# First layer of a two-layer kernel: the channel mixing moved from the input of the big product to its result

## The reference, cut to what matters

```python
agg_w = einsum('bk,koi->boi', att, weight[..., 0])     # one 64 x 64 matrix per batch
agg_b = att @ bias_k                                   # one number per batch and channel
xf    = einsum('boi,bih->boh', agg_w, x) + agg_b[:, :, None]
h     = relu(layernorm(xf @ gw1.T + gb1)); gates = h @ gw2.T + gb2; top 2 of 8, capacity
out   = x + xf @ weight.T + lora(xf, gates)            # tmp = xf @ lora_A
# second layer: convolution along the 1024, condition bias, products with Wq, Wk, W, A, mixed experts
```

## Time and profile before

| what | value |
|---|---|
| median of 3 runs | 1356.77 us (1352.99 to 1357.81) |
| profiled execution | 1357.82 us, of it the span of the trace 1356.0 |
| PE busy | 1305.2 us (96%), mean granted clock 0.987 |
| DVE busy | 814.2 us (60%); 7 or 8 tenths in phase A, 4 or 5 in phase B |
| ACT, POOL busy | 301.2 us (22%), 243.4 us (18%) |
| DMA | mean 93 GB/s over the span |

### The profile page before, as it was taken

The page is one execution under the profiler, slowest core; times in us unless marked ns, Lnnn a source line. Parts: engine busy times, 40 slices in busy tenths (PEclk is TensorE's granted clock), DMA queues, the critical chain, the costliest instruction groups (busy, mean ns, idle before and its releaser), DMA issues.

```text
span 1356.0 us, 21754 instructions
## 1 busy us (share of the span) xinstructions
PE 1305.2 (96%) x7429; PEld 1206.8 (89%) x7429; DVE 814.2 (60%) x2039; ACT 301.2 (22%) x510; POOL 243.4 (18%) x145
## 2 busy tenths in 40 slices
PE   6799999999999997879999999999999999999999
PEld 6699999999999996768988988989889889898897
DVE  7888888888888885545454454454544544545442
ACT  5422332223322331311111111111111111111110
POOL 5422223222222222400100101001001010010010
PEclk9899999999999998889999999999999999999999
DMA  5422222232222235542443433524434335244320
GB/s 200 168 71 90 86 70 70 73 100 72 70 70 90 85 87 160 163 98 67 99 99 73 109 82 84 113 68 99 100 75 106 83 84 112 69 100 98 80 52 31
DMA packets 100295, 125.74 MB, mean 93 GB/s; under 512 B 5168, under 2 KB 80944, under 8 KB 100272
## 3 DMA queue, kind: packets, MB, share of 16 engines
q1 hardware_dynamic: 100272, 125.43, 34.5%
HBM read 71.62 MB, written 53.80 MB: 92 GB/s over the span
## 4 chain that ended last, share of the span: by engine, by line
PE 77%; DVE 12%; issue 3%; ACT 3%; DMA 1%; DVEq 0%; ACTq 0%; SPq 0%
PE ps L998 22%; PE ps L999 21%; PE ps L1000 21%; PE ps L1123 6%; PE ps L1041 3%; PE ps L1124 2%; DVE gate L762 2%; ACT row L543 2%; DVE whole L726 2%; DVE whole L729 1%; DVE row L767 1%; PE ps L1042 1%; DVE mixs L707 1%; DMA x_round<-row 1%; ACT lhs_h L534 1%
## 5 line engine op out<-in xcount | busy, mean ns | idle before, releaser
L998 PE MATMUL ps<-weights,lhs_h 128*128 128x396 f32 (+2 forms) x1792 | 635.0, 354 | 11.8 <-DVE row L748 6.0
L999 PE MATMUL ps<-weights,lhs_h 128*128 128x396 f32 (+2 forms) x1792 | 624.9, 349 | 0.0
L1000 PE MATMUL ps<-weights,lhs_l 128*128 128x396 f32 (+2 forms) x1792 | 624.3, 348 | 0.0
L998 PEld LDWEIGHTS ps<-weights,lhs_h 128*128 128x128 f32 x1792 | 339.8, 190 | 36.9 <-issue 11.4
L1000 PEld LDWEIGHTS ps<-weights,lhs_l 128*128 128x128 f32 x1792 | 339.2, 189 | 20.6
L999 PEld LDWEIGHTS ps<-weights,lhs_h 128*128 128x128 f32 x1792 | 339.6, 190 | 19.6
L506 POOL TENSOR_TENSOR xo<-row,on_all 128x512 f32<-128x512 f32 x64 | 84.1, 1339 | 676.1 <-DMA out_x<-xo 669.3
L1123 PE MATMUL ps<-conv_hl,part_h 128*128 128x256 f32 x512 | 123.9, 332 | 2.4 <-DVE part_l L886 2.4
L465 POOL TENSOR_TENSOR part_l<-xo,part_h 128x1024 fp32r<-128x1024 f32 x31 | 83.1, 2681 | 210.5 <-ACT part_h L527 210.5
L1124 PE MATMUL ps<-conv_hl,part_l 128*128 128x128 f32 x512 | 115.3, 225 | 0.0
L534 ACT ACTIVATE lhs_h<-whole 128x512 fp32r<-128x512 f32 x64 | 40.5, 633 | 319.1 <-DVE whole L729 319.1
(11 more groups left out here) (144 smaller groups left out, 1283.0 us busy)
## 6 DMA issues: line engine op xcount, KB each, us to landing
spill<-row SPq DMA_DIRECT2D x32, 584.5 KB, 3.8
row<-spill SPq DMA_DIRECT2D x31, 584.5 KB, 5.8
z<-x_round SPq DMA_DIRECT2D x32, 516.0 KB, 4.0
xo<-in_x SPq DMA_DIRECT2D x32, 512.0 KB, 4.1
x_round<-row SPq DMA_DIRECT2D x64, 256.0 KB, 5.4
out_x<-xo SPq DMA_DIRECT2D x31, 512.0 KB, 2.7
staging<-in_w SPq DMA_DIRECT2D x8, 832.0 KB, 5.5
bias_in<-cond_rows SPq DMA_DIRECT2D x63, 64.0 KB, 3.9
```

The costliest lines, as they stand in the source:

```text
L998: pe.matmul(out_ap, lhs[0], rhs[0], start=first, stop=False, skip_group_check=True)
L999: pe.matmul(out_ap, lhs[0], rhs[1], start=False, stop=False, skip_group_check=True)
L1000: return pe.matmul(out_ap, lhs[1], rhs[0], start=False, stop=last, skip_group_check=True)
```

## The change

- The host lays x out twice: `xt`, transposed in blocks so that a tile of it is `lhs_h`/`lhs_l` after a split, and `xr`, rows of 1184 columns: `gb1`, 128 zeros, and x in the order of `row`.
- `main` of a tile works on plain x. Its three banks are split again (`y_high` by ACT, `y_low` by DVE, into `yh`, `yl`), and `mix(t, k)` multiplies them with the mixing matrix as the stationary operand, three matmuls of 396 columns for each bank, into banks of their own (BM0).
- `column_sums` multiplies each slice of the weights with a matrix of ones while the first tile is computed; ACT keeps the sums (`wsum`), and for each tile makes `biased` = wsum times the channel's bias. POOL's `row_init` adds it to the loaded `xr` in `row`; `evict` (DVE) adds the mixed banks to that. `lhs_a`, `x_keep`, `main_bank` and the x bias load go.
- `x_low` moves from POOL to DVE; the split of chunk N_LB0 moves from DVE to POOL; the five aside chunks are spread over tiles 1 to 5.
- The condition's small matmuls stand between the slices of tile 0, on PE and ACT; the warming matmuls ahead of tile 0 are gone.

The core of the diff (blank lines left out):

```diff
-        BY0 = (4, 5, 7)
+        BY0, BM0, BC = (4, 5, 7), (1, 2, 3), (0, 6)
...
-        by_pool = (3, 6, N_CONV, N_LB1, N1, N1 + 1, N1 + 2, N1 + 4, N1 + 6)
+        after0 = {N1 + 2: last0 - 2, N1 + 3: last0 - 1, N1 + 5: last0}
+        by_pool = (3, 6, N_LB0, N_CONV, N_LB1, N1, N1 + 1, N1 + 2, N1 + 4, N1 + 6)
...
-        aside = {0: (N_LB0, N_CONV), 1: (N_LB1, N1), TILES - 2: (N1 + 1,)}
+        aside, HEAD = {1: N_LB0, 2: N_CONV, 3: N_LB1, 4: N1, 5: N1 + 1}, 6
...
+            def load_xt(t, u):
+                sp.dma_start(xo[:, u, :], a["xt"][bass.ts(t, P), :]).then_inc(xt_in[u], 16)
+            def load_xr(t, u):
+                sp.dma_start(row[:, u, 0:OUT0], a["xr"][bass.ts(t, P), :]).then_inc(xr_in[u], 16)
...
+            load_xt(0, 0)
+            chunk(0)
             sp.dma_start(cbuf[:, 0:CPACK], a["cpack"]).then_inc(cond_in, 16)
+            chunk(1)
+            chunk(2)
...
+            chunk(3)
+            load_xt(1, 1)
+            chunk(4)
...
+            sp.wait_ge(*low_of(3))
+            load_xr(0, 0)
...
+                once, ahead, thrice = counts(t + 1, t + 3, t * 3 + 3)
+                if later(t, 1) and before_end(t, 1):
+                    left, = counts((it + u) * 16)
+                    sp.wait_ge(spilled[1 - u], left)
                     sp.sem_inc(passed_sp, 1)
...
+                    load_xr(t + 1, 1 - u)
+                if before_end(t, 4):
+                    sp.wait_ge(x_lo, ahead)
+                    sp.sem_inc(passed_sp, 1)
+                    load_xt(t + 4, u)
+                if isinstance(t, int) and t + 1 in aside and t > 0:
+                    chunk(aside[t + 1])
...
+                sp.wait_ge(mix_read, thrice)
+                sp.sem_inc(passed_sp, 1)
+                sp.wait_ge(counted, once)
+                sp.sem_inc(passed_sp, 1)
+                sp.dma_start(spill[bass.ts(t, P), :], row[:, u, HG:END]).then_inc(spilled[u], 16)
...
+            def row_init(t, u, it):
+                pool.wait_ge(biased_ready, t + 1)
+                pool.wait_ge(xr_in[u], it * 16 + 16)
+                if later(t, 1):
+                    pool.wait_ge(counted, t)
+                pool.tensor_tensor(row[:, u, 0:OUT0], row[:, u, 0:OUT0], biased[:, :], ALU.add).then_inc(row_ready, 1)
...
+                if before_end(t, 1):
                     mix_product(t + 1)
...
+                    row_init(t + 1, 1 - u, it + u)
+                if isinstance(t, int) and t in aside:
+                    split_lo(aside[t])
...
             def x_high(t, u, it):
...
+                act.wait_ge(xt_in[u], it * 16 + 16)
...
+                    act.wait_ge(main_done, t * 3 - 3)
+                act.activation(lhs_h[:, u, :, :], xo[:, u, :].rearrange("p (j t) -> p j t", j=J),
+                               ACT.Copy).then_inc(x_hi, 1)
+            def y_high(t, k):
+                act.wait_ge(main_done, t * 3 + k + 1)
+                if later(t, 1):
+                    act.wait_ge(mix_done, t * 3 - 2 + k)
+                act.activation(yh[:, k, :], ps[:, BY0[k], 0:BANK0], ACT.Copy).then_inc(y_hi, 1)
+            def bias_of(t):
+                if later(t, 1):
+                    act.wait_ge(row_ready, t)
+                    act.sem_inc(passed_act, 1)
+                act.activation(biased[:, :], wsum[:, 0:OUT0], ACT.Copy,
+                               scale=aggc[:, bass.ds(t, 1)]).then_inc(biased_ready, 1)
...
+            x_high(0, 0, 0)
+            split_hi(0)
...
+            act.activation(h1, ps[:, BC[0], 0:B], ACT.Gelu, bias=cb0).then_inc(cond_act, 1)
+            split_hi(1)
...
+            split_hi(4)
             x_high(1, 1, 0)
...
+            for k in range(3):
+                act.wait_ge(wsum_done, k + 1)
+                act.activation(wsum[:, BANK0 * k:BANK0 * k + BANK0], ps[:, BM0[k], 0:BANK0],
+                               ACT.Copy).then_inc(wsum_ready, 1)
+            y_high(0, 0)
+            y_high(0, 1)
+            act.wait_ge(aggc_ready, 2)
+            act.wait_ge(wsum_ready, 3)
+            bias_of(0)
...
+            def phase_a(t, u, it):
+                if at(t, TILES - 1):
+                    root(t)
+                    y_high(t, 2)
+                    return
+                y_high(t, 2)
+                if before_end(t, 2):
+                    x_high(t + 2, u, it + 1)
+                y_high(t + 1, 0)
+                bias_of(t + 1)
+                root(t)
+                y_high(t + 1, 1)
+                if isinstance(t, int) and t in aside:
+                    split_hi(aside[t])
...
+            def x_low(t, u):
+                dve.wait_ge(x_hi, t + 1)
+                dve.tensor_tensor(lhs_l[:, u, :, :], xo[:, u, :].rearrange("p (j t) -> p j t", j=J),
+                                  f32(lhs_h[:, u, :, :]), ALU.subtract).then_inc(x_lo, 1)
+            def y_low(t, k):
+                dve.wait_ge(y_hi, t * 3 + k + 1)
+                dve.tensor_tensor(yl[:, k, :], ps[:, BY0[k], 0:BANK0], f32(yh[:, k, :]),
+                                  ALU.subtract).then_inc(y_lo, 1)
...
+            def evict(t, u, k):
+                dve.wait_ge(mix_done, t * 3 + k + 1)
+                if k == 0:
+                    dve.wait_ge(row_ready, t + 1)
...
+                dve.tensor_tensor(row[:, u, lo:hi], ps[:, BM0[k], 0:hi - lo], row[:, u, lo:hi],
+                                  ALU.add).then_inc(mix_read, 1)
...
+                y_low(t, 2)
+                if before_end(t, 2):
+                    x_low(t + 2, u)
+                evict(t, u, 0)
+                y_low(t + 1, 0)
+                evict(t, u, 1)
+                evict(t, u, 2)
+                if at(t, TILES - 2):
+                    mix_matrix(t + 1)
                 route(t, u)
-                if at(t, 1):
-                    links["n"] += MIX_LINKS
+                y_low(t + 1, 1)
+                if not at(t, TILES - 2):
+                    mix_matrix(t + 1)
...
-            main_bank(TILES - 1, 1, 1)
+            evict(TILES - 1, 1, 1)
+            evict(TILES - 1, 1, 2)
...
+            def cond(step):
+                if step == 0:
+                    pe.wait_ge(cond_in, 16)
+                    pe.matmul(ps[:, BC[0], 0:B], cw0, emb_t, start=True, stop=True).then_inc(cond_pe, 1)
+                elif step == 1:
+                    pe.wait_ge(cond_act, 1)
+                    pe.matmul(ps[:, BC[1], 0:B], cw1, h1, start=True, stop=True).then_inc(cond_pe, 1)
+                elif step == 2:
+                    pe.wait_ge(cond_act, 2)
+                    pe.matmul(ps[0:B, BC[0], 64:64 + KATT], h2, cw2, start=True, stop=True).then_inc(cond_pe, 1)
+                elif step == 4:
+                    pe.wait_ge(consts_in, 16)
+                    pe.wait_ge(cond_dve, 4)
+                    pe.transpose(ps[0:KATT, BC[1], 64:64 + B], att, eye[0:B, 0:B]).then_inc(cond_pe, 1)
+                    pe.matmul(ps[0:B, BC[1], 128:128 + C], emb_t, ctx_w, start=True, stop=True).then_inc(cond_pe, 1)
+                    pe.matmul(ps[:, BC[0], 128:128 + TILES * KATT], batch_part, wbuf[0:B, 0:TILES * KATT],
+                              start=True, stop=True).then_inc(cond_pe, 1)
+                elif step == 6:
+                    pe.wait_ge(cond_dve, 6)
+                    pe.matmul(ps[:, BC[1], 192:192 + B], bias_k, attT, start=True, stop=True).then_inc(cond_pe, 1)
...
+            def column_sums(j):
+                for k in range(3):
+                    for s in range(2):
+                        mm = pe.matmul(ps[:, BM0[k], 0:BANK0], ones[:, :], w0[:, k, j, s, :],
+                                       start=(j == 0 and s == 0), stop=(j == J - 1 and s == 1), skip_group_check=True)
+                    if j == J - 1:
+                        mm.then_inc(wsum_done, 1)
...
+                if j0 == 0 and k == 0:
+                    pe.wait_ge(x_hi, t + 1)
...
+                    pe.wait_ge(y_lo, t * 3 - 2 + k)
...
+            def mix(t, k):
+                if k == 0:
+                    pe.wait_ge(mix_ready, t * 2 + 2)
+                pe.wait_ge(y_lo, t * 3 + k + 1)
+                if later(t, 1):
+                    pe.wait_ge(mix_read, t * 3 - 2 + k)
+                elif k == 0:
+                    pe.wait_ge(wsum_ready, 3)
+                split_product(ps[:, BM0[k], 0:BANK0], (mix_h, mix_l), (yh[:, k, :], yl[:, k, :])).then_inc(mix_done, 1)
+            pe.wait_ge(zeroed, 4)
+            for j in range(J):
+                for k in range(3):
+                    main(0, 0, k, j, j + 1)
+                column_sums(j)
+                cond(j)
...
+                main(t + 1, 1 - u, 0)
+                for k in range(3):
+                    mix(t, k)
+                main(t + 1, 1 - u, 1)
+                if at(t, TILES - 2):
+                    mix(t + 1, 0)
+                main(t + 1, 1 - u, 2)
...
+    rows = f["x"].reshape(B * C, D)
+    a = {"xt": rows.reshape(TILES, P, J, P).transpose(0, 3, 2, 1).reshape(TILES * P, D),
```

(2 more changed lines are left out.)

424 lines of the change are left out of this document (121 added, 303 removed).

## The result

The changed kernel takes 1365.24 us (median of 6 runs, 1361.14 to 1366.87) where the kernel before takes 1357.32 beside it (6 runs): a ratio of 1.0055, 95% interval 1.0034 to 1.0077. Measured again later (e16) it was 1.0053 (1.0039 to 1.0067). The change costs some 7.5 us; I had forecast a gain of 7.3.

What follows compares the result with a forecast made beforehand. PE was taken to bound phase A, with DVE just behind. `x1_add` moving from 531.55 to 523.3, less 1 us, gave 7.3 us off the profiled 1357.8: 1350.5, or 1349.5 as a median; range 1341 to 1363.

Steps and rivals of the forecast that it cites:

- A tile on PE: Steady tile of phase A: 81 matmuls at 0.181 us, 14.65 us, 0.6 us less than before.
- What is late in a tile: Steady tile of phase A: DVE has the next matrix at 16.6 us, PE wants it at 19.0; 2.4 us of slack.
- DVE's round: DVE's time per phase A tile: 10.6 us of work plus 3.3 us of blocks by POOL, 13.9 us.
- The aside tiles: Tiles 1 to 5, with extra POOL work inside DVE's routing: PE waits between 0 and 9 us, 4 taken.
- The start: Tile 0's slices in series with the condition, slices 0 and 2 at half clock: tile 1 starts at about 50.7 us, against 43.06.
- the bound of 53: Late bound for tile 1's start, in us, with half clock in slice 1 too.
- The end: Tile 31 to phase B: starts at 494.6, gates at 24 to 27.5 us, `x1_add` after 28.7, at 523.3 against 531.55.
- From there on the chains are the same: Behind `x1_add`: nothing changes except SP's queue ahead of tile 0's store, 1 us added (0 to 2).
- Only phase A and its two ends can move: Phase B's code is unchanged, so its time was held for equal.
- Rivals 2: The start is free: blocks at 60%, no half clock in slice 2; 1343 us, chance 0.19.
- rival 4: Phase A: DVE becomes the bound once blocks exceed 4.05 us a tile; 1360 to 1370 us, chance 0.15.
- Rival 3: The gain is eaten: POOL blocks DVE fully in the aside tiles, half clock in slice 1; 1357 us, chance 0.21.

Runs made afterwards that it cites:

- e16: The changed kernel itself, unedited, measured again beside later runs: 1.0053 of the kernel before.
- e7: The changed kernel without the wait of POOL's `row_init` for the tile's count: 1.0021 of the kernel before.
- e13: The changed kernel with 28, 38 and 24 small matmuls filling PE's gaps behind start slices 0, 1 and 4: 0.9992 of the kernel before.
- e1: The changed kernel with POOL's memset of z, SP's padding stores, tile 0's row and two w1 chunks issued one or two tiles earlier: 1.0019 of the kernel before.
- e2: The changed kernel with tile 0's row load and two w1 chunks put ahead of the memset wait and padding stores in SP's order: 1.0011 of the kernel before.
- e6: The kernel of e1 with POOL's low part of w1 chunk N1+2 held until tile 0's gates have written tmpw: 0.9998 of the kernel before.
- e14: The changed kernel with the edits of e1, e3, e5, e6 and e7, and w1 chunk N1+4 issued behind z's load: 0.9887 of the kernel before.
- e3: The changed kernel with ACT's high splits of w0 slices 1 and 2 moved ahead of the condition activations: 0.9995 of the kernel before.
- e5: The kernel of e1 with a w1 chunk, tile 0's store and its z load ahead of SP's waits for tile 31's routing and spill: 0.9981 of the kernel before.
- e10: The changed kernel with 28, 60 and 50 small matmuls filling PE's gaps behind start slices 0, 1 and 4: 1.0051 of the kernel before.

## Why the prediction was wrong, by its own steps

- **A tile on PE: right.** 81 matmuls at 0.181, 14.65 us forecast, 14.64 from the mix of tile 29 to that of tile 30; PE never waits between 200 and 500 us.
- **What is late in a tile: right in its verdict, wrong in its picture.** PE doesn't wait for DVE. The block that I put into routing lies on the matrix (L716, 1.84 us for two instead of 0.41), because `row_init` waits for the count. e7 made my picture true and PE was as little touched. DVE's round was mis-sized: 13.9 us forecast, 11.4 measured (232.54 of 300 us), of which the blocks take 2.0 (1.4 at L716, 0.6 at `x_low`) and not 3.3.
- **The aside tiles: near.** 4 us forecast, 1.0 + 1.6 = 2.6 us of waits measured, at 133.14 and 149.66.
- **The start: mechanism right, a term mis-sized.** "I count slice 2 at half clock" at 2.25 us; it was slices 1, 2 and 5, and e13 prices them at 6.1 us. The idle 2.98 us ahead of slice 1 was in my own sum (14.3 plus 2.6 against the end of slice 0) and I gave it no cost. Tile 1 started at 54.3, 1.3 past the bound of 53.
- **The end: the step that failed.** "The gates at 24 to 27.5, depending on POOL's split of the first w1 chunk". The chain of DVE nearly held: routing of tile 31 ended 22.3 us after the tile's start, forecast 21 to 22. But I costed SP's and POOL's instructions there only by how long they hold others, not by when they can start. Tile 0's row was late for a memset that was moved behind a new wait; no term of the sum had it, and e1, e2 and e7 show it, the gates waiting for the row in none of them. `x1_add` came 34.9 us after the tile's start, forecast 28.7: 6.2 us. e1 takes back 3.4 of them, since POOL's split, which I had in the range of the gates, then falls on the routing; e6 and e7, where it doesn't, reach 27.9 and 28.6. "From there on the chains are the same ... I add 1 us (0 to 2)": it was 4.4 to z, 1.2 of it the store's own wait and 3.2 its longer way behind the chunk. I had seen the chunk in the queue and priced it too low: with the chunk alone moved behind it, e14 shows 2.7.
- **"Only phase A and its two ends can move": wrong by 1.8 us.** Phase B is longer by 0.07 us a tile.

The miss from 1349.5 to 1365.2 is 15.7 us: start 3.6, asides -1.4, tile 0's row 6.2, from `x1_add` to z 3.4 beyond the forecast, the steady tiles of phase B 1.8, its opening and last tile 0.6, and 1.3 because the profiled execution lies 1.05 above the median of the kernel before and 0.25 below that of the changed one. That is 15.5, and 0.2 stay in the rounding. Rivals 2 and 4 are ruled out: the start was not free, and PE never waited for DVE in the steady tile, though the measured time lies among the 1360 to 1370 us of rival 4. Rival 3 (1357 us) had one thing right, the half clock of slice 1, and not the aside tiles. That the end could turn into a wait for transfers was none of my rivals.

What stays open: what makes a tile of phase B 0.07 us longer. Averaged over 26 tiles, no single one of the 142 steps that the traces hold of a tile differs by more than 0.012 us, PE has no idle time in either, and shifts of the arrays by 16 or 32 bytes changed nothing. Open too is what decides when PE falls to half clock in a start like this one.

## What to carry to other kernels

When an instruction is moved or a wait is added on a side engine, follow everything issued behind it to the end of the phase, the one-off work of the last tiles above all: here a memset of 1 us behind a wait that cost nothing for 30 tiles held the gates for 6 us. For a stretch where PE has several short pieces with gaps between them, put a sum at half clock beside the one at full clock: the length of a gap alone did not tell which it would be. Filling the gaps with matmuls that end in time gave back 6 us, and too many of them gave nothing. Price a chain's gains in their combination: holding POOL's split and storing first each gained alone, and the one undid the other until the chunk was moved too.

## What the runs showed of the hardware that I had not expected

I had counted POOL's blocks only on operations with two SBUF inputs. In these rows others are stretched as well, each until POOL's operation ends: the cast of 64x64 (L716) from 0.41 us for two to 1.84, and to 5.45 in an aside tile; a `TENSOR_SCALAR` of 32 columns from 0.30 to 1.52. The reduction L713 was not (0.67 and 0.68 us, beside `row_init` and without). The Trainium skill (SBUF — State Buffer, section "SBUF: two separate sides") names a two-port mode as the other way into the lock. The trace fits this, with the cast at 1.84 us beside POOL's operation, but does not show which operation ran in such a mode. For the smallest, a difference of one column with two SBUF inputs (L761), the lock made 3.65 us out of 0.16.

After idle times of 2.86 to 4.43 us PE restarted at 1.2 GHz in each of the three cases in the start of the changed kernel; after 0.40 us at 2.4. But the length of the idle time does not settle it. Slice 5 of e3 restarted at 1.2 GHz after 2.25 us and slice 3 of the same kernel at 2.4 after 2.79; the conv of e5, after 3.31 us, began at full clock and fell to half after its first 14 matmuls; and tile 1 of e3 and e10 fell to half after an idle time of 1.82 us. With the 90 short matmuls of e13 in the gaps every slice behind slice 0 ran at full clock.
